# Relu of a key difference in place of two key parts for one head in two, and a fused sum-and-maximum on VectorE

## The reference

```python
scores = jnp.einsum('blhd,bshd->bhls', q, k) / math.sqrt(D_HEAD)
weights = jax.nn.softmax(scores, axis=-1)
out = jnp.einsum('bhls,bshd->blhd', weights, v)
```

## Time and profile before

| | |
|---|---|
| median of 3 runs | 3439.08 us (3438.27 to 3440.1) |
| profiled execution, first to last instruction | 3437.2 us |
| TensorE busy / VectorE busy / ScalarE busy | 3289.5 / 2955.9 / 2473.5 us |
| exponentials (L957) | 4096, mean 599 ns |
| takes of maxima (L981) | 2928, mean 885 ns |
| a query group in mid-kernel | 38.16 us |

### The profile page before, as it was taken

One profiled execution on the slowest core, in us unless ns is written; L12 is line 12 of the kernel. 1 busy time (PEld: TensorE's weight loads), 2 busy tenths in 40 slices (PEclk: granted clock), 3 DMA queues, 4 the chain that ended last, 5 costly groups with the idle time before them and its releaser, 6 DMA issues. The chain is left out here.

```text
span 3437.2 us, 66173 instructions
## 1 busy us (share of the span) xinstructions
PE 3289.5 (96%) x25137; PEld 1521.3 (44%) x25138; DVE 2955.9 (86%) x4695; ACT 2473.5 (72%) x4700; POOL 580.5 (17%) x601
## 2 busy tenths in 40 slices
PE   8999999999999999888899889999999999999997
PEld 5433333333333333567677656533333333333332
DVE  8889999999999997353787665499999999999991
ACT  4178888888888888533333324688888888888886
POOL 4410000000000000053331143133333210000001
PEclk9689999999999999889999999999999999999999
DMA  8451220202021100345010376513132231202001
GB/s 270 138 140 47 41 39 15 44 16 39 15 44 32 24 15 5 129 135 191 27 36 12 121 248 200 139 35 58 35 52 45 52 64 27 44 16 40 15 16 49
DMA packets 306934, 232.77 MB, mean 68 GB/s; under 512 B 205591, under 2 KB 257720, under 8 KB 301970
## 3 DMA queue, kind: packets, MB, share of 16 engines
q1 hardware_dynamic: 290308, 179.45, 22.6%
q0 software_dynamic: 14832, 47.79, 4.3%
q10 hardware_dynamic: 1504, 1.64, 0.1%
HBM read 126.49 MB, written 102.76 MB: 67 GB/s over the span
## 5 line engine op out<-in xcount | busy, mean ns | idle before, releaser
L957 ACT ACTIVATE att_l_probs<-att_l_s_ps 128x512 f32<-128x512 f32 x4096 | 2142.0, 599 | 309.5 <-PE att_l_s_ps L900 269.3
L981 DVE TENSOR_REDUCE att_in_part_max<-att_l_max_ps 128x1 f32<-128x512 f32 (+1 forms) x2928 | 2292.0, 885 | 9.9 <-PE att_l_max_ps L890 9.5
L915 PE MATMUL att_l_o_ps<-att_l_probs,att_l_v_sb 128*17 128x512 f32 (+2 forms) x11776 | 1171.5, 470 | 1.4 <-DMA att_l_v_sb<-v_rows 1.1
L900 PE MATMUL att_l_s_ps<-att_in_q_sb,att_in_k_sb 50*128 50x512 f32 x2048 | 734.4, 453 | 10.1 <-DVE att_l_o_ps L995 9.0
L900 PE MATMUL att_l_s_ps<-att_in_q_sb,att_l_k_sb 50*128 50x512 f32 x2048 | 727.0, 453 | 1.3
L890 PE MATMUL att_l_max_ps<-att_l_k_sb,att_in_q_sb 50*128 50x512 f32 x2048 | 722.4, 445 | 5.2 <-DVE att_in_part_max L981 5.2
L890 PE MATMUL att_l_max_ps<-att_in_k_sb,att_in_q_sb 50*128 50x512 f32 x1856 | 660.0, 449 | 5.0 <-DVE att_in_part_max L981 4.8
L890 PEld LDWEIGHTS att_l_max_ps<-att_l_k_sb,att_in_q_sb 50*128 50x128 f32 x2048 | 336.2, 184 | 319.7 <-DVE att_in_part_max L981 297.8
L900 PEld LDWEIGHTS att_l_s_ps<-att_in_q_sb,att_l_k_sb 50*128 50x128 f32 x2048 | 328.6, 184 | 267.5 <-ACT att_l_probs L957 238.4
L900 PEld LDWEIGHTS att_l_s_ps<-att_in_q_sb,att_in_k_sb 50*128 50x128 f32 x2048 | 335.1, 186 | 241.3 <-ACT att_l_probs L957 202.3
L890 PEld LDWEIGHTS att_l_max_ps<-att_in_k_sb,att_in_q_sb 50*128 50x128 f32 x1856 | 307.8, 186 | 290.5 <-DVE att_in_part_max L981 268.4
(11 more groups left out here) (264 smaller groups left out, 2758.3 us busy)
## 6 DMA issues: line engine op xcount, KB each, us to landing
att_in_q_sb<-q_hi SPq DMA_DIRECT2D x256, 64.0 KB
slot_rows<-att_l_zeros POOLq DMA_DIRECT2D x10, 1024.0 KB, 4.5
ffn_parts<-slot_rows SPq DMA_DIRECT2D x40, 256.0 KB, 3.1
tile_out<-ffn_parts SPq DMA_DIRECT2D x40, 256.0 KB, 2.2
att_in_q_sb<-q_lo SPq DMA_DIRECT2D x128, 72.0 KB
att_l_v_sb<-v_rows SPq DMA_DIRECT2D x16, 544.0 KB, 15.2
att_in_k_sb<-k_hi SPq DMA_DIRECT2D x32, 256.0 KB, 8.9
att_l_k_sb<-k_hi SPq DMA_DIRECT2D x32, 256.0 KB, 9.4
```

The costliest lines, as they stand in the source:

```text
L900: nc.tensor.matmul(s_ps[:, c % SB], k_sb[j // GPB % 2][rows, pair, u * P:(u + 1) * P], q_sb[rows, j % QR, pair], start=True, stop=True).th ...
L915: last = nc.tensor.matmul(o_ps[32 * h:32 * h + AUG, c0:c1], v_sb[:, j // GPB % 2, u, h * AUG:(h + 1) * AUG], probs[:, (n * KT + u) % PB, h ...
L957: nc.scalar.activation(probs[:, (n * KT + u) % PB, h], s_ps[:, c % SB], ACT.Exp, scale=float(HD) ** -0.5).then_inc(exp_done, 1)
L981: nc.vector.reduce_max(dst, banks, AX.X).then_inc(units_taken, 1)
```

## The change

The maximum over key parts 2 and 3 is written differently for one of the two heads of a pair. With a = q.k2 and b = q.k3 for two keys that lie 512 apart, max(a, b) = a + relu(b - a), and b - a = q.(k3 - k2). The projections now also make `rise`, the difference of key parts, split in high and low and stored in DRAM; `load_keys` loads it (NK from 6 to 9 DMAs). In every period unit 5 is the product with `rise`. It goes to the scores' ring `s_ps` as a ninth entry (between exponentials 4 and 5), and ScalarE applies Relu to it into `above` (SBUF). Unit 7 is the product with part 2; VectorE adds `above` to it and takes the maximum in one instruction, `tensor_tensor_reduce`. The six takes become five: single, double, single, double, fused. The first 48 steps of the maxima (`first_maxima`) are as before, except that the halves are stored the other way round; the parts no longer written are set to a very low number once.

```diff
-NQ, NK, NSH = 16 * 6, 16 * 6, 16 * 2 * NSHIFT
+NQ, NK, NSH = 16 * 6, 16 * 9, 16 * 2 * NSHIFT
+RISE_HALF = 0
+BELOW = -3.0e38
...
+    rise_hi, rise_lo = heads_of(io.rise_hi), heads_of(io.rise_lo)
+    for row0, dram in ((0, rise_hi), (HD, rise_lo), (SHIFT0 + NSHIFT, rise_hi)):
+        src = dram[ds(it, 1), g, RISE_HALF].rearrange("a c p t -> (a c) p t")[:, :, T // 2 - G:T // 2]
+        eng.dma_start(rise[:].bitcast(F32)[row0:row0 + HD], src).then_inc(ai.k_loaded[g % 2], 16)
...
+RISE_AT, BASE_AT = 5, 7
+PART_OF = (0, 0, 1, 1, 2, 3, 3, 2)
+HELD = tuple(i for i in range(UNITS) if i != RISE_AT)
-TAKES = ((0,), (1, 2), (3,), (4,), (5, 6), (7,))
+TAKES = ((0,), (1, 2), (3,), (4, 5), (6,))
...
+        def acts_before(p):
+            return UNITS * p + min(p, PERIODS)
+        def rise_act(p):
+            return acts_before(p) + RISE_AT
+        def exp_act(n, u, h):
+            w, c = u // STEP_TILES, u % STEP_TILES * HG + h
+            p = period_of(n, w)
+            return acts_before(p) + c + (p < PERIODS and c >= RISE_AT)
...
+                if i == RISE_AT:
+                    c = rise_act(p)
+                    pe.wait_ge(exp_done, c - SB + 1)
+                    nc.tensor.matmul(s_ps[:, c % SB], q_sb[rows, j % QR, pair, tile * P:(tile + 1) * P],
+                                     rise_sb[j // GPB % 2][rows, pair], start=True, stop=True).then_inc(s_ready, 1)
+                    return
+                held = HELD.index(i)
+                if held >= MB:
+                    pe.wait_ge(units_taken, p * len(TAKES) + TAKE_OF[held - MB] + 1)
+                elif p > 0:
+                    before = max(x for x in range(len(HELD)) if x % MB == held)
+                    pe.wait_ge(units_taken, (p - 1) * len(TAKES) + TAKE_OF[before] + 1)
+                nc.tensor.matmul(max_ps[:, held % MB], q_sb[rows, j % QR, pair, tile * P:(tile + 1) * P],
                                  k_sb[j // GPB % 2][rows, pair, part * G:(part + 1) * G], start=True, stop=True).then_inc(unit_ready, 1)
             def scores(n, j, u, h):
-                c = n * EXPS + u * HG + h
+                c = exp_act(n, u, h)
...
+            def take_rise(p):
+                if p >= PERIODS:
+                    return
+                c = rise_act(p)
+                act.wait_ge(s_ready, c + 1)
+                if p > 1:
+                    act.wait_ge(units_taken, (p - 1) * len(TAKES))
+                nc.scalar.activation(above[:, p % 2], s_ps[:, c % SB], ACT.Relu).then_inc(exp_done, 1)
...
+                        if u % STEP_TILES * HG + h == RISE_AT:
+                            take_rise(period_of(n, u // STEP_TILES))
                         exps(n, u, h)
...
+                if HELD[units[0]] == BASE_AT:
+                    dve.wait_ge(exp_done, rise_act(p) + 1)
+                    nc.vector.tensor_tensor_reduce(above[:, p % 2], max_ps[:, units[0] % MB], above[:, p % 2], 1.0, BELOW,
+                                                   ALU.add, ALU.max, part_max[:, g % 2, first:first + 1]).then_inc(units_taken, 1)
+                    return
```

In layer 0's projection GpSimd gets six more operations for each pair of groups (and its loop is written out), and SyncE four more stores:

```diff
+                for a in range(2):
+                    nc.gpsimd.tensor_tensor(rise[:, a], whole[:, 1, 2 + a], whole[:, 0, 2 + a], ALU.subtract).then_inc(rise_ready, 1)
+                pool.wait_ge(rise_ready, i * 2 + 2)
+                if i > 0:
+                    pool.wait_ge(rise_stored, i * (16 * 4))
+                for a in range(2):
+                    nc.gpsimd.tensor_copy(rise_parts[:, a, 0], rise[:, a]).then_inc(rise_hi_ready, 1)
+                pool.wait_ge(rise_hi_ready, i * 2 + 2)
+                for a in range(2):
+                    nc.gpsimd.tensor_tensor(rise_parts[:, a, 1], rise[:, a], rise_parts[:, a, 0].bitcast(F32), ALU.subtract).then_inc(rise_lo_ready, 1)
```

In layer 1's, GpSimd does ten operations for each batch (`take_rise(b)`, from the fourth group's parts) before that batch's scatter, SyncE stores the result behind the fourth group's parts and values, and ScalarE's split of the fifth group's keys waits for GpSimd's first reads:

```diff
             for b in range(B):
+                take_rise(b)
                 pool.wait_ge(put_ready, b + 1)
...
+                if q == GPB - 1:
+                    store_rise(b)
...
+                if n >= GPB and a >= 2:
+                    act.wait_ge(parts_read, 4)
```

More of the change, by code:

```diff
@@ L256, in first_maxima @@
             rows = slice(half * HROWS, half * HROWS + XROWS)
-            last = nc.tensor.matmul(ps[:, k % 2 * 2 + half], ai.q[rows, j, pair, tile * P:(tile + 1) * P],
+            last = nc.tensor.matmul(ps[:, k % 2 * 2 + 1 - half], ai.q[rows, j, pair, tile * P:(tile + 1) * P],
                                     ai.k[0][rows, pair, part * G:(part + 1) * G], start=True, stop=True)
@@ L408, in store_group, with store_rise @@
                         sync.dma_start(dst, parts[:, slot, a, part].bitcast(F32)).then_inc(stored[slot], 16)
+            def store_rise(i, b, pair):
+                for a in range(2):
+                    sync.wait_ge(rise_lo_ready, i * 2 + a + 1)
+                    for part, dram in enumerate((io.rise_hi, io.rise_lo)):
+                        dst = dram[ds(b, 1)].rearrange("a h c t -> (a h) c t")[:, a * (HD // 2):(a + 1) * (HD // 2), ds(pair * G, G)]
+                        sync.dma_start(dst, rise_parts[:, a, part].bitcast(F32)).then_inc(rise_stored, 16)
             with sync.Fori(0, GPB // 2) as i:
@@ L438, in _ @@
             pool.wait_ge(ln.z_ready, TPG)
-            set_shift_rows(nc, ai.k[0], ai)
-            pool.wait_ge(ai.rows_set, 2)
-            with pool.Fori(0, PAIRS_OF) as i:
+            set_shift_rows(nc, ai.k[0], ai.rise[0], ai)
+            pool.wait_ge(ai.rows_set, 3)
+            for i in range(PAIRS_OF):
                 for slot in range(2):
@@ L877, in maximum @@
                 j, it = g % NB, g // NB
[L878 removed]
+                if k == 0 and i == 0:
                     pe.wait_ge(q_loaded[j % QR], NQ * (it * (NB // QR) + j // QR + 1))
@@ L2009, in store_parts, with store_rise @@
                         sync.dma_start(dst, parts[:, n % 2, a, part].bitcast(F32)).then_inc(stored[n % 2], 16)
+            def store_rise(b):
+                for a in range(2):
+                    sync.wait_ge(rise_lo_ready, b * 2 + a + 1)
+                    for part, dram in enumerate((io.rise_hi, io.rise_lo)):
+                        dst = dram[ds(b, 1)].rearrange("a h c t -> (a h) c t")[a * NHH:(a + 1) * NHH, :, T // 2 - G:T // 2]
+                        sync.dma_start(dst, rise_parts[a][:, part].bitcast(F32)).then_inc(rise_stored, 16)
             for n in range(N):
@@ L2049, in _, with take_rise @@
             sync.wait_ge(v_stored, N * 16)
+            sync.wait_ge(rise_stored, B * 16 * 4)
         @block.gpsimd
         def _(pool):
+            def take_rise(b):
+                n = b * GPB + GPB - 1
+                first, second = parts[:, 0].bitcast(F32), parts[:, 1].bitcast(F32)
+                for a in range(2):
+                    done = b * 2 + a
+                    pool.wait_ge(lo_ready, n * 4 + 2 + a + 1)
+                    if done > 0:
+                        pool.wait_ge(rise_lo_ready, done)
+                    for part in range(NPART):
+                        nc.gpsimd.tensor_tensor(rise[:, part], second[:, 2 + a, part], first[:, 2 + a, part], ALU.subtract).then_inc(parts_read, 1)
+                    pool.wait_ge(parts_read, done * 2 + 2)
+                    nc.gpsimd.tensor_tensor(rise[:, 0], rise[:, 0], rise[:, 1], ALU.add).then_inc(rise_step, 1)
+                    pool.wait_ge(rise_step, done + 1)
+                    if b > 0:
+                        pool.wait_ge(rise_stored, b * 16 * 4)
+                    nc.gpsimd.tensor_copy(rise_parts[a][:, 0], rise[:, 0]).then_inc(rise_hi_ready, 1)
+                    pool.wait_ge(rise_hi_ready, done + 1)
+                    nc.gpsimd.tensor_tensor(rise_parts[a][:, 1], rise[:, 0], rise_parts[a][:, 0].bitcast(F32), ALU.subtract).then_inc(rise_lo_ready, 1)
             nc.gpsimd.memset(va[:].rearrange("p t (h c) -> p (t h) c", c=AUG)[:, :, HD:AUG], 1.0).then_inc(ones_set, 1)
```

87 lines of the change are left out of this document (55 added, 32 removed).

## The result

The changed kernel takes **3720.69 us** (median of 4 runs, 3718.85 to 3724.23), in the same comparison as 3439.59 before: a ratio of 1.0817, 95% interval 1.0802 to 1.0832. The forecast was 3747, 26 us too high. The profiled execution, the slowest of the four (3724.23), spans 3722.5 us, 285.3 more than before.

The account below looks back on a forecast made before the run. VectorE and a TensorE-ScalarE loop of 4.66 us were taken as bounds nearly abreast; the relu lengthens the latter. 3437.2 + 296 (attention) + 12 (projections) = 3745 us of span, plus 1.9 to the median: 3747, range 3640 to 3850.

Parts of the forecast that it names:

- What bounds the changed kernel: Scores' ring: score 7 waits for the relu's end, +0.69 us, with the value block still behind it.
- Period 5.35: Regular attention period with maxima: 4.66 us plus 0.69 from score 7's later issue gives 5.35 us.
- the sum: Attention's added time over 61 groups: 43.01 us a group in place of 38.16, in all +296 us.
- X: VectorE's time for the fused add-and-maximum, taken as 0.75 us; hidden unless above 0.87.
- VectorE's loop: From unit 2's product, waiting for the previous fused take, round to that take: 4.48 + X = 5.23 us, hidden by 0.12.
- The second loop: VectorE's loop through the maxima's bank 2, forecast at 5.23 us, hidden by 0.12 us under the relu's period.
- loop 2: Later name for VectorE's loop: unit 2's product waits for the previous period's last take; forecast 4.48 + X.
- Projections, +12: GpSimd operations, stores and loads for the difference: +1 us in layer 0, +11 in layer 1 (4 to 24).
- B: ScalarE: the relu costs only one pitch, 0.48 us, so 90 us less, 3657; chance 0.08.
- C: VectorE: the fused take becomes the bound, 1.24 us long, period 5.72, total 3928; chance 0.11.
- D: ScalarE: each relu swaps the activation table, 1283 ns twice a period, about 5000 us; chance 0.02.
- E: ScalarE's 0.40 us of idle absorbs the relu and VectorE's relief counts: 3400 us, faster; chance 0.04.

Follow-up runs that it names:

- e10: Changed kernel with VectorE's takes reordered to double, double, single, single, fused: 3842.27 us, ratio 1.1165.
- e11: Changed kernel with a plain maximum for the fused take, relu on 64 of 512 columns, and takes double, double, single, single, single: 3675.24 us.
- e4: Changed kernel with the fused take made a plain maximum of the same bank, same waits: 3720.95 us, ratio 1.0819.
- e1: Changed kernel with the relu moved from ring entry 5 to entry 3 of the period's nine: 3708.71 us, ratio 1.0785.
- e3: Changed kernel without the relu and its product, the last take a plain maximum, projections unchanged: 3514.39 us, ratio 1.0219.
- e5: Changed kernel with a plain maximum for the fused take and the relu reading 64 of 512 columns: 3688.80 us, ratio 1.0723.
- e6: Changed kernel with the last 512-column value block cut in two, half of it ahead of pair 7: 3701.30 us, ratio 1.0764.
- e7: Kernel before the change with the last 512-column value block cut in two, half ahead of pair 7: 3511.88 us, ratio 1.0212.
- e9: Kernel before the change with six more GpSimd operations per pair of groups in layer 0's projection, on an unread scratch tile: 3450.84 us, ratio 1.0032.
- e2: Changed kernel with the relu moved from ring entry 5 to entry 1 of the period's nine: 3961.28 us, ratio 1.1518.
- e12: Changed kernel with the relu as ring entry 3 and takes double, double, single, single, fused: 3837.76 us, ratio 1.1152.

## Why the prediction was right, by its steps

**What bounds the changed kernel.** Right. Score 7 waits for the relu's end and the value block stands behind it. Three results carry this: e10 (the relu 0.30 later, the period 0.30 longer), e10 against e11 (shortening the relu counts almost whole), and e4 (the fused take does not matter).

**Period 5.35.** Measured 5.27. Its terms: relu 2.62 after exponential 0 (forecast 2.69), 0.60, 0.05 for the signal (0.09), 2.00 to exponential 0 (1.97). I took the start of today's exponential 5 for the relu's; its product went 2.08 after exponential 0 (2619.27) where I had 2.12, and the relu started 0.54 behind it where I had 0.57. The first period is 5.48 (forecast 5.56; 2606.36 to 2611.84), the second 5.35. Group: 42.44 in place of 43.01, so 0.57 x 61 = 35 us too much in the sum. The attentions are 258.9 us longer where the sum had 296.

**X and VectorE's loop.** X was taken as 0.75 of VectorE's time. The pass is 0.68 long, of which the next instruction overlaps 0.07, and the accumulator read takes 0.08: 0.69. VectorE's loop is then 4.48 + 0.69 = 5.17, and the changed kernel shows it hidden: the fused take's read ends at 2622.13 + 0.08 = 2622.21, and unit 2 goes only at 2622.44, 0.18 later than it could with 0.05 for the signal. The rule of the Trainium skill's "VectorE: DVE Perf Modes" (Two Vector instructions with no wait between them), that an accumulator output is a second instruction, is seen here; the trace agrees, with 488 of 83 ns.

**The second loop in the experiments.** The prediction had it, 0.12 below the first (5.27 against e5's 5.19 measured), and my expectations of e1, e3 and e5 did not use it. With it e5's 5.19 comes out, and half of e1's periods; e6's miss is the shifted wait of score 6. The prediction has that wait in VectorE's loop ("when exponential 4 is done and score 6 goes"), but I did not carry it over to e6. e7's miss is the price of the cut. For e3 the prediction's form of loop 2 gives 4.48 + 0.61 less one exponential's 0.48, so 4.61, and 4.84 was measured: there unit 5's product went 0.29 after score 6 (2621.76, 2622.05), where it goes beside it in the changed kernel. Unit 5 lies on the same half of the array's rows as score 5, and follows it by 0.34 (2621.71, 2622.05), as unit 6 follows score 6 on the other half by 0.34 (2621.76, 2622.10). In the changed kernel score 6 waits for exponential 4 and goes 0.49 after score 5 (2619.32, 2619.81), so the half is free again. That the half is the reason is read from these distances; no run tests it.

**Projections, +12.** Measured +26.3. Layer 0: forecast +1, measured +11.3. I had asked only whether GpSimd's idle time has room for its six operations, and not what they do to VectorE while they run; e9 shows that. The Trainium skill's "GPSIMD Engine Reference" (Key points) says that GpSimd shares its SBUF interfaces with VectorE, with contention where VectorE runs in a 2-port mode or reads two SBUF inputs. Four passes of L137 took 3.63 us in place of 1.38, so the trace agrees that there is contention and gives its price. L137 reads one SBUF tensor, so by the page it has to be in a 2-port mode; no row shows the mode. Layer 1: forecast +11, measured +15.0, within its bounds of 4 and 24; no run takes this stage apart.

**The balance.** 35 us too much in the periods (37 by the stages), 14 too little in the projections: 23 us, the difference between 3745 and 3722.5 of span. That the total is closer than the attentions' sum is luck: the two errors have opposite signs.

**The rivals.** B (pitch only, 3657): false, the relu's end counts. C (the fused take as bound): false, X = 0.69. D: false; the changed kernel has 18 table loads, as many as the one before, and none between an exponential and a relu. The Trainium skill's "ScalarE: Activation LUTs" (Table sets) says that relu is in every set, and the trace agrees. E (absorbed, 3400): false, and e3 shows more, that even without a relu these five takes, in this order, are not faster. It is this part of the change that I had not priced by itself: a period of 4.84 against 4.66.

## What to carry to other kernels

When an entry goes into a ring, list the waits of every later entry with its new partner, and not only the one that is on the path now: here score 7, score 6 and (in e2) score 2 each got another partner, and in one kernel or another each of these waits stood in the loop that set the period. A second loop that stands 0.1 us below the first sets the size of every later improvement, so it belongs into each estimate. And taking work off an engine that is abreast with two others buys nothing if the work's order changes: a take over two units starts only when the later one is there, and so it can hold up a product that stands ahead of the critical one on TensorE (e2, e10, e12).
